# A Mamba2 and two feed-forward layers in one kernel: batch 1's dt step one stage earlier, both residual sums on VectorE, the last tile in halves

## The reference

```python
res = x
h = rmsnorm(x, ln1_w)
h = res + mamba2(h, w_in, conv_w, conv_b, A_log, D, dt_bias, w_out)
res = h
h2 = rmsnorm(h, ln2_w)
mlp = silu(h2 @ gate_w.T) * (h2 @ up_w.T) @ down_w.T
x = layernorm(x + res + mlp)                      # x + the block's own output
# second layer, weights rounded to -1, 0, 1 times a scale
x = layernorm(x + ((x @ g.T) * (x @ u.T)) @ d.T)
```

## Time and profile before

| | us |
|---|---|
| median of 3 runs | 478.28 (476.49 to 478.68) |
| the profiled execution, whole | 479.27 |
| its span, first to last instruction | 477.4 |
| PE busy | 462.0 (97%) |
| DVE busy | 336.8 (71%) |
| ACT busy | 259.6 (54%) |
| GpSimd busy | 232.7 (49%) |
| mean granted clock of TensorE | 0.995 of 2.4 GHz |

### The profile page before, as it was taken

How to read it: one execution, slowest core, us unless ns; L and a number is a source line. 1 busy time by engine, 2 the same in 40 slices (tenths; PEclk the granted TensorE clock), 3 DMA queues, 4 the chain that set the end, 5 groups by cost and what they waited for, 6 DMA issues and landing times.

```text
span 477.4 us, 6373 instructions
## 1 busy us (share of the span) xinstructions
PE 462.0 (97%) x2068; PEld 370.6 (78%) x2068; DVE 336.8 (71%) x581; ACT 259.6 (54%) x508; POOL 232.7 (49%) x283
## 2 busy tenths in 40 slices
PE   7998979999999989999999999999999999999995
PEld 7886757776777768888878888888887777788883
DVE  3674465774677797766798899984968665587274
ACT  4889647868657666557333334322618765658000
POOL 5483555435673398776887400017028455652022
PEclk9999989999999999999999999999999999999999
DMA  8720212112232305435323326620110010000022
GB/s 241 246 89 1 89 44 67 45 44 89 89 90 88 133 0 199 141 125 168 120 89 132 125 92 223 212 98 1 44 45 0 1 45 23 1 1 1 0 89 88
DMA packets 14432, 40.81 MB, mean 85 GB/s; under 512 B 2368, under 2 KB 2368, under 8 KB 14400
## 3 DMA queue, kind: packets, MB, share of 16 engines
q1 hardware_dynamic: 14400, 40.41, 25.2%
HBM read 38.30 MB, written 2.10 MB: 85 GB/s over the span
## 4 chain that ended last, share of the span: by engine, by line
PE 83%; DVE 7%; ACT 6%; issue 3%; POOL 2%; POOLq 0%; DVEq 0%; ACTq 0%
PE psA L1723 6%; PE psA L1725 6%; PE psA L1738 6%; PE psA L1740 5%; PE psA L1731 3%; PE psA L1729 3%; PE psB L1934 3%; PE psB L1930 3%; PE psB L1933 3%; PE psB L1740 2%; PE psB L1738 2%; PE psB L2033 2%; PE psB L2021 2%; PE psB L2032 2%; PE psB L2022 2%
## 5 line engine op out<-in xcount | busy, mean ns | idle before, releaser
L799 POOL TENSOR_SCALAR var<-mv 128x1 f32<-128x1 f32 x16 | 4.5, 280 | 107.7 <-DVE mv L1299 107.6
L861 POOL TENSOR_TENSOR beta<-wsum,beta 128x512 fp32r<-128x512 f32 x28 | 36.2, 1313 | 20.9 <-ACT beta L1066 20.9
L1188 ACT ACTIVATE c<-c 128x512 f32<-128x512 f32 x14 | 8.9, 632 | 47.4 <-DVE c L1525 47.4
L1711 PE MATMUL psA<-xT_h,win_h 128*128 128x512 f32 x80 | 32.1, 401 | 0.0
L1712 PE MATMUL psA<-xT_l,win_h 128*128 128x512 f32 x80 | 31.2, 391 | 0.0
L1425 DVE SCALAR_TENSOR_TENSOR xbc<-psA,convw_sb,xbc 128x511 f32<-128x511 f32 (+2 forms) x36 | 26.9, 747 | 4.3 <-ACT xbc L1125 3.4
L1198 ACT ACTIVATE act_hl<-act 128x512 fp32r<-128x512 f32 x28 | 17.0, 627 | 18.5 <-PE psB L1934 12.2
L990 POOL TENSOR_TENSOR int_l<-int,int_h 128x512 fp32r<-128x512 f32 x11 | 14.3, 1296 | 17.9 <-ACT int_h L1269 17.9
L1723 PE MATMUL psA<-xT_h,beta 128*128 128x512 f32 x56 | 22.0, 393 | 1.0 <-DVE tT_l L1346 0.7
L1575 DVE TENSOR_TENSOR act_hl<-act,act_hl 128x512 fp32r<-128x512 f32 x28 | 19.0, 686 | 3.9 <-ACT act_hl L1198 3.9
L1725 PE MATMUL psA<-xT_l,beta 128*128 128x512 f32 x56 | 21.8, 389 | 0.0
(11 more groups left out here) (337 smaller groups left out, 1603.3 us busy)
## 6 DMA issues: line engine op xcount, KB each, us to landing
raw<-in_f_gu_t SPq DMA_DIRECT2D x22, 512.0 KB, 3.4
raw<-in_w_gu_t SPq DMA_DIRECT2D x14, 512.0 KB, 3.7
raw<-in_f_dn_t SPq DMA_DIRECT2D x10, 512.0 KB, 3.3
raw<-in_w_gu_t SPq DMA_DIRECT2D x14, 256.0 KB, 2.7
raw<-in_w_dn_t SPq DMA_DIRECT2D x7, 512.0 KB, 3.3
raw<-in_w_in_t SPq DMA_DIRECT2D x5, 512.0 KB, 4.0
x<-in_hidden SPq DMA_DIRECT2D x8, 256.0 KB, 4.9
out<-x SPq DMA_DIRECT2D x8, 256.0 KB, 2.0
```

Of the source, the lines that this page charges most:

```text
L861: nc.gpsimd.tensor_tensor(beta[:, f % 2, 1, cols], wsum[:, f % 2, cols], beta[:, f % 2, 0, cols].bitcast(F32), ALU.subtract).then_inc(gb_l ...
L1711: nc.tensor.matmul(ps, sh, mh, start=i == 0, stop=False)
```

## The change

The step dt(1) moves from behind inproj(0,9) to behind inproj(0,8), ahead of chunk (0,0); dtturn(1) and dtlog(1) move from behind chunk (0,1) to behind inproj(0,9); dtend(1) stays behind chunk (0,1). The xsum steps go. DVE makes both sums behind outproj from the bank: nrm = bank + x, then x = 2x + bank; the bank is free after the second, and ACT's square waits for the first by the semaphore sum_taken. In the step with p1(9) (s = NX + NZ - 1), tlow(3) goes ahead of tlast(2) and the waits for t_low change with it; `before` was the xsum step alone there and is empty now. The product, the sum, the statistics, the scaling and the store of the last tile are made in two halves of 256 columns, in two banks.

```diff
@@ -70,8 +70,6 @@
                 decay.append(("until", b, r + 1))
-            if r >= 2:
-                decay.append(("xsum", b, r - 2))
             leave = [("outproj", b, r - 1)] if 1 <= r <= NC else []
@@ -100,8 +98,10 @@
             steps.append(load("out", j - NX - 1))
+        if j == NX + NZ - 2:
+            steps.append(("dt", 1))
         if j == NX + NZ - 1:
-            steps.append(("dt", 1))
+            steps += [("dtturn", 1), ("dtlog", 1)]
         steps += after + [("conv", 0, j)] + last
@@ -114,7 +114,7 @@
         if j == 0:
-            steps += [("dtturn", 1), ("dtlog", 1), ("dtend", 1)]
+            steps.append(("dtend", 1))
         steps += ([("conv", 1, j)] if convolve else []) + last
@@ -144,8 +144,8 @@
-            steps += first + [("gsplit", 0, 0)] + before + after + held[:1] + thigh + held[1:] + [("tlow", *turned)]
-            steps += second + [("p1", NPRE - 1), ("gsplit", 0, 1)]
+            steps += first + [("gsplit", 0, 0)] + after + held[:1] + thigh + [("tlow", *turned)] + held[1:]
+            steps += second + [("p1", NPRE - 1), ("gsplit", 0, 1)] + before
         elif s == SCAN_ACT:
@@ -291,9 +291,7 @@
     for c in range(NC):
-        steps += [("ffndown1", c), ("ffnsum", 1, c)]
-        if c >= 1:
-            steps.append(("ln2", 1, c - 1))
+        steps += [("ffndown1", c), ("ffnsum", 1, c)] + ([("ln2", 1, c - 1)] if c else [])
     steps.append(("ln2", 1, NC - 1))
@@ -350,7 +348,7 @@
         elif kind == "ffndown1":
-            b.append(("ffndown", 1, *at))
+            b += [("ffndown", 1, *at)] + ([("ffndown", 1, NC)] if at[0] == NC - 1 else [])
         elif kind == "down" and at[1] == 0:
@@ -515,7 +513,7 @@
         y_ready = sem("y_ready")
-        u_ready = sem("u_ready")
+        sum_taken = sem("sum_taken")
         acth_ready = sem("acth_ready")
@@ -563,6 +561,7 @@
         bn_ready = sem("bn_ready")
+        half_summed = sem("half_summed")
         ln1_ready = sem("ln1_ready")
@@ -707,6 +706,7 @@
+        halves_of_tile = [slice(0, D // 2), slice(D // 2, D)]
         TERN = [n for n, w in enumerate(LOADS) if w[0] in ("qgu", "qdn")]
@@ -778,10 +778,13 @@
                     sp.dma_start(ln2_sb[:], ln2_w.to_broadcast([P, D])).then_inc(ln2_loaded, 16)
-            for t in range(NT):
+            for t in range(NT - 1):
                 sp.wait_ge(out_ready, t + 1)
                 sp.dma_start(out[t], x[:, t, :]).then_inc(out_stored, 16)
-            sp.wait_ge(out_stored, 16 * NT)
+            for i, cols in enumerate(halves_of_tile):
+                sp.wait_ge(out_ready, NT + i)
+                sp.dma_start(out[NT - 1, :, cols], x[:, NT - 1, cols]).then_inc(out_stored, 16)
+            sp.wait_ge(out_stored, 16 * (NT + 1))
@@ -955,11 +958,6 @@
                     reciprocal_deviation(step, sq[:, i:i + 1], 1.0 / D)
-                elif kind == "xsum":
-
-                    t = tile_of(step)
-                    pool.wait_ge(nrm_ready, NC + t + 1)
-                    nc.gpsimd.tensor_tensor(x[:, t, :], x[:, t, :], nrm[:, t % 2, :], ALU.add).then_inc(u_ready, 1)
                 elif kind in ("ln1", "ln2"):
@@ -1161,8 +1159,7 @@
                     t = tile_of(step)
-                    s.wait_ge(*freed_b(step))
-
+                    s.wait_ge(sum_taken, t + 1)
                     nc.scalar.activation(yt_h[:], nrm[:, t % 2, :], ACT.Square,
@@ -1322,7 +1319,7 @@
                     if c >= 1:
-                        v.wait_ge(t_low, 2 * c)
+                        v.wait_ge(t_low, 2 * c + (c == NC - 1))
                     nc.vector.tensor_tensor(t_f[:, 3], t_f[:, 1], xT_f[:, 0:2, chunk(c)], ALU.subtract)
@@ -1485,10 +1482,11 @@
                         v.wait_ge(*done_b(("dtturn", t)))
-                    else:
-                        v.wait_ge(u_ready, t - 1)
-                    nc.vector.tensor_tensor(nrm[:, t % 2, :], bank_b(step), x[:, t, :], ALU.add)\
-                        .then_inc(freed_b(step)[0], 1)
+                    nc.vector.tensor_tensor(nrm[:, t % 2, :], bank_b(step), x[:, t, :], ALU.add).then_inc(sum_taken, 1)
+                    v.wait_ge(sum_taken, t + 1)
+
+                    nc.vector.scalar_tensor_tensor(out=x[:, t, :], in0=x[:, t, :], scalar=2.0, in1=bank_b(step),
+                                                   op0=ALU.mult, op1=ALU.add).then_inc(freed_b(step)[0], 1)
                 elif kind == "norm2":
@@ -1595,7 +1593,6 @@
                     v.wait_ge(*completed(job))
-                    v.wait_ge(u_ready, t + 1)
                     nc.vector.tensor_tensor(x[:, t, :], bank_of(job), x[:, t, :], ALU.add).then_inc(freed(job)[0], 1)
@@ -1673,6 +1670,19 @@
                         .then_inc(int_low[1], 1)
+                elif step == ("ffnsum", 1, NC - 1):
+                    t = tile_of(step)
+                    v.wait_ge(ln1_ready, t + 1)
+                    for i, cols in enumerate(halves_of_tile):
+                        job = ("ffndown", 1, at[1] + i)
+                        v.wait_ge(*done_b(job))
+                        nc.vector.scalar_tensor_tensor(out=x[:, t, cols], in0=bank_b(job)[:, cols],
+                                                       scalar=scl[:, 13:14], in1=x[:, t, cols], op0=ALU.mult,
+                                                       op1=ALU.add).then_inc(half_summed, 1)
+                        v.wait_ge(half_summed, i + 1)
+                        v.wait_ge(bn_ready, NT + t)
+                        link(nc.vector.bn_stats(bn6[:, i, :], x[:, t, cols]))
+                    nc.vector.bn_aggr(mv[:, NT + t, :], bn6[:]).then_inc(bn_ready, 1)
                 elif kind == "ffnsum":
@@ -1688,8 +1698,9 @@
                     v.wait_ge(rstd_ready, i + 1)
-                    nc.vector.tensor_scalar(x[:, t, :], x[:, t, :], mv[:, NT + t, 0:1], rstd[:, i:i + 1],
-                                            ALU.subtract, ALU.mult).then_inc(out_ready, 1)
+                    for cols in halves_of_tile if t == NT - 1 else [slice(0, D)]:
+                        nc.vector.tensor_scalar(x[:, t, cols], x[:, t, cols], mv[:, NT + t, 0:1], rstd[:, i:i + 1],
+                                                ALU.subtract, ALU.mult).then_inc(out_ready, 1)
@@ -1893,7 +1904,7 @@
                     f = at[0]
-                    pe.wait_ge(t_low, 2 * NC - 1)
+                    pe.wait_ge(t_low, 2 * NC - 2)
                     pe.wait_ge(gb_low, 2 * f + 1)
@@ -2022,6 +2033,18 @@
                             done.then_inc(b_done, 1)
+                elif step == ("ffndown1", NC - 1):
+
+                    c = at[0]
+                    for i, cols in enumerate(halves_of_tile):
+                        ps = open_b(("ffndown", 1, c + i))
+                        for f in range(FF):
+                            high, low = int_parts(1, f)
+                            nc.tensor.matmul(ps[:, cols], high[:, chunk(c)], q_dn[:, f, cols], start=f == 0,
+                                             stop=False)
+                            done = nc.tensor.matmul(ps[:, cols], low[:, chunk(c)], q_dn[:, f, cols], start=False,
+                                                    stop=f == FF - 1)
+                        done.then_inc(b_done, 1)
                 elif kind == "ffndown1":
```

## The result

The changed kernel takes **471.92 us** (median of 4 runs, 471.72 to 472.54), the kernel before 477.38 (4 runs, the three ahead and one more, 476.29 to 478.68). The ratio is 0.988, 95% interval 0.985 to 0.991: faster, by 5.5 us. The forecast was 471.6, its range 469.8 to 474.8. The profiled execution took 472.09 us, with a span of 470.2 against 477.4. Those 7.2 us between the two profiles are more than the medians' 5.5; e9 says why.

What follows compares the result with a forecast made beforehand. PE, busy 462.0 of 477.4 us, was taken as the bound, with only idle time and slow stretches to gain. -0.55 - 3.26 - 1.61 + 1.15 - 1.7 - 0.7 = -6.67 us from the median 478.28 gave 471.6, range 469.8 to 474.8.

Steps and rivals of the forecast that it cites:

- The dt move: Batch 1's dt matmuls ahead of chunk (0,0): -0.55 us; the wait at the first output projection goes: -3.26 us.
- the bank order: outproj(0,0), still psB's job 19, follows xb(0,1) instead of cb(0,1), so its 3.26 us wait goes.
- The slow clock: At the first output projection, the slow clock goes with the wait: 4.33 us becomes 2.72, -1.61 us.
- The second sums: DVE's added sum behind outproj, 0.79 us per tile; 1.15 us reach norm2(0,2), whose turn PE awaits: +1.15 us.
- one more table load: ACT loads Exp and Ln for dt and Exp again for chunk (0,1): 1.28 us more, costed at nothing.
- The t steps: GpSimd's sums gone and tlow(3) ahead of tlast(2) shorten PE's waits around the end of t: -1.7 us.
- sign on L1327: Sign that the forecast is right: L1327 takes 0.4 to 1.0 us where it was 1.52.
- The last tile: Last tile in halves: its matmuls cost nothing extra, and the tail behind the last one shortens by 0.70 us.
- the split at nothing: Last tile's 44 matmuls of 256 columns, priced at 0.111 us each from the state products: 4.9 against 5.0.
- Rival 3: Weight loads bind in the last tile's 44 matmuls: +3.4 us, 475.0; chance 0.05.

Runs made afterwards that it cites:

- e9: The kernel before, unchanged, in three more single executions a, b and c: 476.36, 476.62 and 478.99 us.
- e1: The changed kernel with dt of batch 1 back at its old place: 478.61 us, ratio 1.001 to the kernel before.
- e5: The changed kernel with one more, unused Ln on ACT behind the Exp of chunk (0,1), forcing table loads: 473.26 us.
- e3: The changed kernel with the second residual sum back on GpSimd for both batches: 473.69 us.
- e10: The changed kernel with the old order of the steps around t(2) and t(3), tlow behind tlast: 471.96 us.
- e8: The changed kernel with the last tile's two parts as 384 and 128 columns: 472.75 us.
- e4: The changed kernel with the last tile in one piece again, 22 matmuls of 512 columns: 472.19 us.
- e7: The changed kernel with DVE's a22 steps of parts 1 and 2 behind its sum of p7(0): 471.13 us.
- e6: The kernel before with 27 unused transposes keeping PE busy in the wait ahead of outproj(0,0): 477.46 us against 479.85, ratio 0.995.

## Why the prediction was right, and where not

1. **The dt move: right in size; the mechanism right, its two parts wrongly weighed.** -0.55 and -3.26 forecast, together -3.81, and -3.65 measured; no wait, and a start at 59.25 where about 59.7 was forecast (T came 0.74 earlier). The step gives the credit to the bank order, and that is the smaller part. In the kernel before, the projection started 1.27 behind decay(0,1) (62.37 to 63.64); with the old bank it could have started at about 58.41 + 1.27 = 59.68 here, an estimate from these rows, only 0.43 later than it did. The other 2.8 of the 3.26 come from the decay, which no longer stands behind a dt chain that waits for ACT's Ln. No run moved one without the other.
2. **The slow clock: -1.61 forecast, -1.61 in the two profiles, but not in each execution.** The step took one trace's stretch for a property of the kernel. Where the clock stays up (e9 a and b) the term is -0.1, and the whole change is worth 474.5 - 470.2 = 4.3 us between spans, or 5.0 with T set equal.
3. **The second sums, +1.15: wrong, 0 instead.** The step failed where the dt part costed ACT's "one more table load". It saw the load that is added (dt's own Exp, at 50.18 in ACT's timeline after) and not the one for chunk (0,2) that goes (at 75.15 before); from chunk (0,0)'s Exp to chunk (0,2)'s there are five loads in either kernel. It had counted the loads of the moved step and not the table that it leaves behind. The gaps from which 1.15 was made hold with dt in its old place (0.96 in e1) and with a forced load (1.10 in e5). The price of one sum, 0.79 forecast, was 0.72.
4. **The t steps, -1.7: -1.91 at p7(0), then +0.92.** The cause was right (GpSimd's sums, e3); the part of it that the step put down to the moved tlow was not tlow's (e10). What the step lacked is what comes next: it ended at p7(0) and didn't ask what DVE's next instructions, the two a22, would run beside once GpSimd's work had moved. Net -0.99. Its sign on L1327 (now L1324), 0.4 to 1.0 instead of 1.52, held at tile (1,1) with 0.42 and not at the last tile, where the same step takes 1.51 and took 0.95 before.
5. **The last tile, 0 and -0.70: +0.29 and -0.52.** 44 matmuls came 0.120 apart, 5.27 us for all against 4.98; the 0.111 of the earlier trace rows is what 128 columns take, as e8 shows, and 256 take 0.009 more. Behind the last matmul the sum's step took 0.52 where 0.45 was forecast, the statistics to the next start 0.46, and the two scalings together 0.73. Net -0.23; by the last distance it is 0.22 against e4 and 0.03 against the kernel before, so a third of the 0.70 at most. The term at fault is the split at nothing: it priced 256 columns by rows of 128. Rival 3 falls for 256 columns. By the sentence of the Trainium skill, TensorE: Matmul & The Clock Gate, The mechanism, that the prediction quotes, loads would not overlap here; the trace disagrees, as loads of 0.19 us lie beside matmuls that start every 0.120. The same section also says that a load into the background weight buffer is pulled ahead of running matmuls, and that fits the trace.
6. **The sum.** -6.67 forecast. Measured from T on: -3.65 - 1.61 - 0.18 - 1.91 + 0.92 - 0.03 = -6.46. That is 0.2 from the forecast by luck: the terms of the sums and of the t steps came out 1.33 and 0.21 better than forecast, and p4(0), the tail and the dt move 0.92, 0.67 and 0.16 worse. Taken from a median of 478.28 the forecast fell 0.3 below the result, and part of that closeness is luck too: the median before is itself a mixture of two groups.

## What to carry to other kernels

- When a step with its own activation function is moved, follow the table to the next user behind the old place and the new one. The load that goes may be far from the step, and may pay for something else.
- A change that shifts DVE's or GpSimd's work changes what lies beside what: follow the queue one product beyond the last wait that you remove. Behind it here stood two 256-column steps that nobody needed yet, and moving them (e7) was worth 0.8 us by medians and 0.9 by distance, more than the split tile or the new order.
- Take profiles of several executions before pricing a slow clock: a wait can cost its clock in a part of the runs only (three of five traces here), and then a profile and a median are not of the same thing.

## What was not expected of the hardware

- After one and the same wait of 3.1 us the granted clock fell in three traces (before, e1, e9 c) and stayed in two (e9 a and b). In the three, the 30 first matmuls of the kernel took 6.42, 6.16 and 6.24 us; in the two, 4.98 and 5.15. Five traces don't make that a rule, and why it would be so is open. e6's own profile had 5.10 there, so its evidence is in its five runs' clocks, not in that profile. The Trainium skill, TensorE: Matmul & The Clock Gate, Part 1, says that the watching of PE's activity runs on by itself and isn't set back by the kernel, so that the moment of a change is chance from run to run; the traces agree with that as far as five go.
- The idle time in a wait's row is not what the wait costs PE: 0.76 at p4(0) is 0.92 by distance (e7); in e5 0.35 is 0.61, 0.23 is 0.15, and another 0.34 has no idle time in any row of the matmuls. The distance between starts decides.
- fp32r matmuls with a new weight each follow each other after 0.227 us with 512 columns, 0.173 with 384, 0.120 with 256 and 0.111 with 128 (e8).
- DVE's subtraction of two SBUF tiles of 128x256 took 0.38 where GpSimd idled until 178.10 in the kernel before (0.75 for two, from 177.80), 1.51 in t34(3), and 2.38 for two at the a22 steps. The Trainium skill, SBUF — State Buffer, SBUF: two separate sides, has the two engines hold a shared pair of ports for a whole instruction each. The trace agrees: GpSimd's first subtraction runs from 170.34 for about 1.32 (its group's mean), to 171.66; 0.4 later would be 172.06, and DVE's second a22 ends at 169.71 + 2.38 = 172.09.
